# Entry writes behind the slot's last values, block 0's gather first, and products of zeros on TensorE in the loading phase and among the closing steps

## The chip, the cores and the metric

The kernel runs on one core of a Trainium2 chip, in one launch. The metric is the device time of an execution in microseconds; the median of three runs stands for a kernel. The engines are named as in the profile: PE (TensorE's products) and PEld (its weight loads), DVE (VectorE), ACT (ScalarE), POOL (GpSimd) and SP (SyncE, which here only starts transfers).

## The reference, cut to what matters

The input x is 128 sequences of 32 rows of 256 numbers; each sequence has a context of 257 rows. Six layers follow each other, each added to its input. LN is a layer norm without weights.

```python
x = x + cross_attention(LN(x), ctx)            # one head of 256, softmax, divided by sqrt(256)
x = x + causal_self_attention(LN(x))           # head of 128
x = x + ffn(LN(x))                             # 256 -> 1024 -> 256, quantised weights and activations, gelu
x = x + cross_attention_16_heads(LN(x), ctx)   # heads of 16
x = x + local_attention(LN(x))                 # each row sees two rows on either side
# mixture of experts on x_flat = LN(x), 4096 rows, 8 experts, 2 per row, capacity C = 1280
probs = softmax(x_flat @ router_w.T); top_v, top_i = top_k(probs, 2); top_v /= sum(top_v)
for k in range(2):
    pos = rank of the row among the rows that chose the same expert as k-th choice
    keep = pos < C
    y = gelu(x_row @ w1[e]) @ w2[e]
    out = out + y * (gate * keep)
x = x + out
```

All of it is in float32, apart from the quantised feed-forward layer, whose products run in bfloat16 on whole numbers.

## The kernel before

The 4096 rows are cut into 32 tiles of 128 rows (four sequences each). The kernel has two phases, each a block in which the five engines run programs of their own, tied by semaphores. Between the blocks stands a barrier that all engines pass together (L935).

**The tile phase** (`stack_phase`) is a software pipeline written out by hand. A loop over slots s = -6 ... 35 calls, on each engine, the steps of several tiles in a fixed order: `at(s + 3, c0_scores)` is the first cross-attention's scores of tile s + 3, `at(s, unit_values, 0)` the 16-head attention's values of tile s. That attention works in four units of one sequence each: scores (L1208), row maximum on DVE, exponential on ACT (L1390), transposes (L1216) and values (L1227). The values of a unit are 64 very short products of 128x32 weights with 16 columns, the densest stream of instructions that TensorE has. A unit's last key is not among its products: POOL multiplies it (`unit_last`, L1515) and selects each head's part (`unit_select`, L1520), and DVE adds both (`unit_own`, L808). Values 0 and 1 of a tile stand apart in the slot, values 2 and 3 directly behind each other.

**Routing** goes along in groups of four tiles. DVE works out, over four slots, for each row its two experts, its gates and its two places in a table in HBM. When a group's `place` is done, POOL writes the entries: one indirect DMA for each tile and choice, 128 entries of 8 bytes (`write_entry`, L1536). `tiles_scattered` says in which slot a tile's two writes come. The first five groups, tiles 0 to 19, are written in the tile phase, 40 writes in all; those of the last twelve tiles in the expert phase. In SP's slot 32, the wait for these 40 writes is followed by the load of the first table (`first_places`, L975), from which the first expert blocks take their rows.

**The loading phase** is the first 48 us or so. TensorE multiplies 20 products of zeros (L1024), waits for the first weights, folds Wq and Wk into one matrix (L1028, L1031) and then carries tile 0 through the first cross-attention (`c0_norm_T`, `c0_q`, `c0_scores`, ...), with further folds (`setup_folds`, L1044 and on) behind tile 0's output product. DVE scales and rounds the feed-forward weights in between (L1593, L1598). All the while the contexts of the first four tiles are loaded.

**The expert phase** (`expert_phase`) has 71 blocks of 128 rows, each with one expert: POOL gathers the rows (L2156), TensorE transposes them (`rows_T`, L2016), multiplies with w1 (`up`, L2038), ACT applies the gelu, TensorE multiplies with w2 (`down`, L2025), DVE scales with the gate, and POOL adds the result to the output (L2159). Its first steps are the *closing steps*: the last attention steps of tiles 28 to 31 are called here, woven into blocks 0 to 2. DVE begins with `s1_qT` of tile 30, for which TensorE's first step, `s1_v_scores`, waits; then it adds the last units of tile 31 (`unit_own`) and stages the row numbers of block 0 (`stage_from`, L1908). POOL first does a bias add and the router's inverse deviation and then gathers blocks 0 and 1. SP first starts the w1 weights of blocks 0 and 1 (1 MB each) and the last two experts' w2 (1 MB each).

```python
pe.wait_ge(zero_ok, 1)
for n in range(20):
    mm(ps[:, 6, 0:P], zero[:, 0:P], zero[:, 0:P], start=True, stop=True)
...
for t in tiles_scattered(s):          # POOL: scatter(s - 1, 0), then scatter(s - 1, 1),
    write_entry(t, k)                 # behind unit_select(s + 2, 1)
...
s1_v_scores(tiles - 2)                # TensorE, the first closing steps
unit_fold(tiles - 1, 2)
```

## Time and profile before

| | us |
|---|---|
| median of three runs | 1527.26 |
| lowest and highest | 1524.1, 1529.57 |
| the profiled execution, its own time | 1525.6 |
| its span, first to last instruction | 1523.8 |

| engine | busy us | share of the span | instructions |
|---|---|---|---|
| PE | 1415.4 | 93% | 19592 |
| PEld | 1207.9 | 79% | 19625 |
| DVE | 890.3 | 58% | 3143 |
| ACT | 837.6 | 55% | 2398 |
| POOL | 640.6 | 42% | 1195 |

The durations and times of day in this document are from the profiled execution; times of day count from its first instruction. The tile phase ends at about 961, the expert phase fills the rest. Two shares of the page mislead here. PE's 93% is an average over a phase that it fills and over stretches at half the clock, in which the same work counts double. And the chain that ended last, followed back from the end, names only the last write of the output and covers 0% of the span, so that what bounds must be read from busy times and waits. In the lines of the timeline the first number is the start, the second the length of a group of instructions, and in square brackets stands the idle time of the engine just before it with what ended it; "issue" means that no releaser is known.

### The profile page before, as it was taken

The numbers are of one execution on the slowest core, as the hardware profiler recorded it, in microseconds if no ns is written. First come the engines' busy times: TensorE is split into PE (matmuls) and PEld (weight loads), VectorE is DVE, ScalarE is ACT, GpSimd is POOL, SyncE is SP. The second block draws the span as 40 slices with busy tenths as digits, with TensorE's granted clock in tenths as the row PEclk, the third lists the DMA queues.
The fourth block names the chain that finished last, engine by engine and source line by source line (L and its number), as shares of the span: only waits on it lengthen the run. The fifth ranks groups of instructions, "written<-read, shape, count | busy, mean of one in ns | idle before, by whom it ended". The sixth has DMA issues, their size and how long they took to land. (4 is left out here: it accounts for less than half of the span.)

```text
span 1523.8 us, 51419 instructions
## 1 busy us (share of the span) xinstructions
PE 1415.4 (93%) x19592; PEld 1207.9 (79%) x19625; DVE 890.3 (58%) x3143; ACT 837.6 (55%) x2398; POOL 640.6 (42%) x1195
## 2 busy tenths in 40 slices
PE   6789999999999999999998988799899999999996
PEld 4467878777877777777777766699789999999996
DVE  4668889899988887887887786223211111111111
ACT  0488888888887887887887785322111111111110
POOL 1233444444444444444444343346633434443442
PEclk7999999999999999999999999799999999999999
DMA  9223434343333332332332222466556666666563
GB/s 338 113 68 101 119 98 119 96 123 100 104 105 100 103 96 89 102 107 89 96 99 75 68 86 106 174 172 175 147 171 177 187 187 173 177 186 187 173 176 75
DMA packets 91180, 199.47 MB, mean 131 GB/s; under 512 B 13568, under 2 KB 48128, under 8 KB 79840
## 3 DMA queue, kind: packets, MB, share of 16 engines
q1 hardware_dynamic: 72304, 174.68, 35.9%
q0 software_dynamic: 15680, 18.69, 7.0%
q10 hardware_dynamic: 2992, 3.28, 0.6%
q8 instruction: 140, 2.29, 0.6%
q14 instruction: 64, 0.52, 0.1%
HBM read 178.58 MB, written 18.29 MB: 129 GB/s over the span
## 5 line engine op out<-in xcount | busy, mean ns | idle before, releaser
L2111 ACT ACTIVATE heT<-ps 128x512 f32<-128x512 f32 x142 | 84.8, 597 | 428.3 <-PE ps L2038 401.5
L2038 PEld LDWEIGHTS ps<-xeT,w_block 128*128 128x128 f32 x2272 | 267.5, 193 | 13.5 <-issue 9.5
L2038 PE MATMUL ps<-xeT,w_block 128*128 128x128 f32 x2272 | 269.3, 277 | 9.4 <-DMA w_block<-in_m_w 8.8
L1390 ACT ACTIVATE x_prob<-ps,x_nmax 128x257 f32<-128x257 f32 x512 | 237.3, 473 | 44.9 <-DVE x_nmax L1741 39.8
L2025 PE MATMUL ps<-contexts,heT 128*128 x1136 | 257.0, 379 | 1.6 <-DVE ye L1921 1.6
L2025 PEld LDWEIGHTS ps<-contexts,heT 128*128 128x128 f32 x1136 | 210.3, 190 | 27.6 <-issue 2.0
L1741 DVE TENSOR_REDUCE x_nmax<-ps 128x2 f32<-128x514 f32 x256 | 168.9, 681 | 21.1 <-PE ps L1208 21.0
L1216 PE MATMUL ps<-constants,x_prob 128*128 128x128 f32 x1024 | 159.9, 291 | 12.0 <-ACT x_prob L1390 10.4
L1394 ACT ACTIVATE x_probT<-ps 128x512 f32<-128x512 f32 x256 | 147.2, 631 | 7.4 <-PE ps L1216 6.4
L1920 DVE COPY to_ix<-places 128x1 uint32 x71 | 10.9, 154 | 233.9 <-PE ps L2025 231.3
L1216 PEld LDWEIGHTS ps<-constants,x_prob 128*128 128x128 f32 x1024 | 121.5, 148 | 29.9 <-ACT x_prob L1390 26.2
L1227 PEld LDWEIGHTS ps<-contexts,x_probT 128*32 128x32 f32 x8192 | 97.3, 110 | 59.4 <-issue 36.4
L2153 POOL TENSOR_TENSOR rt_hold<-constants 128x1 f32<-128x1 f32 x145 | 34.8, 240 | 247.5 <-DVE ye L1921 120.3
L1227 PE MATMUL ps<-contexts,x_probT 128*32 128x16 f32 x8192 | 105.4, 185 | 29.0 <-issue 27.9
L2159 POOL DMA_INDIRECT out<-ye,to_ix x71 | 113.5, 1598 | 28.8 <-issue 24.0
L1390 ACT ACTIVATION_READ_ACCUMULATOR x_prob<-ps,x_nmax 128x1 f32 x512 | 103.2, 202 | 0.0
L1515 POOL TENSOR_TENSOR x_lastv<-contexts,x_prob 128x64 f32<-128x64 f32 x128 | 40.6, 317 | 135.9 <-ACT x_prob L1390 130.3
L1208 PE MATMUL ps<-contexts,query_blocks 32*64 32x257 f32 x2048 | 89.0, 403 | 5.4 <-ACT x_probT L1394 3.9
L1939 DVE COPY xeT<-ps 128x256 f32<-128x256 f32 x71 | 30.1, 424 | 97.0 <-PE ps L2016 97.0
L2156 POOL DMA_INDIRECT xe<-xnorm,from_ix x71 | 71.1, 1002 | 22.7 <-issue 20.2
L1520 POOL TENSOR_TENSOR x_select<-constants,x_rinv 128x8 f32<-128x8 f32 x128 | 27.4, 214 | 108.5 <-DVE x_rinv L1745 108.5
L1208 PEld LDWEIGHTS ps<-contexts,query_blocks 32*64 32x64 f32 x2048 | 30.2, 130 | 40.3 <-ACT x_probT L1394 23.5
(282 smaller groups left out, 2938.8 us busy)
## 6 DMA issues: line engine op xcount, KB each, us to landing
w_block<-in_m_w SPq DMA_DIRECT2D x71, 1024.0 KB
contexts<-in_cT SPq DMA_DIRECT2D x112, 257.0 KB, 3.0
contexts<-in_cn SPq DMA_DIRECT2D x112, 256.0 KB, 3.9
contexts<-in_m_w SPq DMA_DIRECT2D x8, 1024.0 KB, 6.9
contexts<-in_cT SPq DMA_DIRECT2D x4, 1028.0 KB, 11.7
xin<-in_x SPq DMA_DIRECT2D x32, 128.0 KB, 2.2
lastq<-in_lastq SPq DMA_DIRECT2D x32, 128.0 KB, 2.3
contexts<-in_cn SPq DMA_DIRECT2D x4, 1024.0 KB, 12.8
```

The costliest lines, as they stand in the source:

```text
L1208: i = mm(ps[h * HS:(h + 1) * HS, r, 0:KEYS], qblk[t % 2][r * GD:(r + 1) * GD, h, u, :, :].rearrange("p e q -> p (e q)"), cT[t % RING][r * ...
L1216: i = tr(ps[:, r, n * P:(n + 1) * P], p1[u % 2][:, r, n * P:(n + 1) * P], ident[:])
L1227: i = mm(b[rows_of, r * DH:(r + 1) * DH], p1T[u % 2][:, r, n, rows_of], cn[t % RING][:, u, n, lo:lo + DH], start=n == 0, stop=n == KT - 1)
L1390: A(p1[u % 2][:, r, :], ps[:, r, 0:KEYS], ACT.Exp, bias=nmax1[u % 2][:, r:r + 1], accum_out=rsum1[u % 2][:, r:r + 1]).then_inc(e1_ok.handl ...
L1394: A(p1T[u % 2][:, 2 * j:2 * j + 2].rearrange("p r k t -> p r (k t)"), ps[:, 2 * j:2 * j + 2, 0:KT * P], ACT.Copy).then_inc(t1_ok.handle, 1)
L1515: tt(lastv[u % 2][:].rearrange("p (r d) -> p r d", r=RG), lastk[t % RING][:, u, :].rearrange("p (r d) -> p r d", r=RG), p1[u % 2][:, :, KE ...
L1741: v_.tensor_reduce(nmax1[u % 2][:, 2 * j:2 * j + 2], ps[:, 2 * j:2 * j + 2, 0:KEYS], AX, ALU.max, negate=True).then_inc(m1_ok.handle, 1)
L2025: t = mm(ps[:, 3, 0:D], heT[b][:, k, :], w2[:, e, k, :], start=k == 0, stop=k == FK - 1)
L2038: t = mm(ps[:, half, at:at + P], w1[b][:, k, f * P:(f + 1) * P], xeT[b][:, k, :], start=k == 0, stop=k == H - 1)
L2111: A(heT[b][:, half * FK // 2:(half + 1) * FK // 2, :].rearrange("p k t -> p (k t)"), ps[:, half, :], ACT.Gelu).then_inc(heT_ok.handle, 1)
L2156: g.indirect_dma_start(xe[b][:], None, sources[round_of(u, n)], bass.IndirectOffsetOnAxis(ap=from_ix[b][:], axis=0)).then_inc(xe_in[b], 16)
L2159: g.indirect_dma_start(sums[round_of(u, n)], bass.IndirectOffsetOnAxis(ap=to_ix[b][:], axis=0), ye[b][:], None, compute_op=ALU.add).then_i ...
```

## The change

Entry writes: POOL's two calls of `scatter` become calls of `scatter_behind`, at two places of the slot: behind `unit_select(s + 1, 3)`, with a wait until TensorE has finished values 3 of that tile, and behind `unit_select(s + 2, 1)`, with a wait for values 0 of tile s + 2. Both writes of a tile come together. `tiles_scattered` gives the first place to all tiles but tile 17, in slots first + 7 to first + 10 of a group; the fifth group is written in three slots, so that its last tile (19) comes in slot 29 and not in 31.

Block 0: DVE stages its rows before it adds units 2 and 3 of tile 31, and POOL gathers it before the bias add and the inverse deviation.

Products of zeros: `keep_busy(n)` issues n products of 128x128 zeros with 256 columns of zeros. In the loading phase these are 10 instead of the 20 narrower ones, 13 behind the first folds, and 3, 1, 1, 1, 1, 1 ahead of tile 0's steps of the first cross-attention. Among the closing steps they are 8, 3, 2, 2, 2, 6 and 2, 25 in all.

```diff
@@ -633,11 +633,14 @@
             if s - (first + n + ROUTED_BEHIND) == turn:
                 return g
 
-    def tiles_scattered(s):
-
-        for first, n in GROUPS[:IN_FIRST]:
-            for i in range(n):
-                if s == first + n + ROUTED_BEHIND + 4 + i:
+    def tiles_scattered(s, early):
+
+        for g, (first, n) in enumerate(GROUPS[:IN_FIRST]):
+            places = [(i, False) for i in range(n)]
+            if g == IN_FIRST - 1:
+                places = [(0, False), (0, True)] + [(i, False) for i in range(1, n - 1)]
+            for i, (turn, first_unit) in enumerate(places):
+                if s == first + n + ROUTED_BEHIND + 4 + turn and early == first_unit:
                     yield first + i
 
     def bank(n):
@@ -1020,8 +1023,11 @@
             mm = nc.tensor.matmul
             tr = nc.tensor.transpose
             pe.wait_ge(zero_ok, 1)
-            for n in range(20):
-                mm(ps[:, 6, 0:P], zero[:, 0:P], zero[:, 0:P], start=True, stop=True)
+            def keep_busy(n):
+                for _ in range(n):
+                    mm(ps[:, 3, 0:D], zero[:, 0:P], zero[:], start=True, stop=True)
+
+            keep_busy(10)
             pe.wait_ge(fold_in, 48)
             for h in range(H):
                 for k in range(H):
@@ -1030,6 +1036,7 @@
                 for k in range(H):
                     t = mm(ps[:, 5, h:h + 1], setup_w["x0_Wk_T"][:, k, h * P:(h + 1) * P], cols["x0_bq"][:, k:k + 1], start=k == 0, stop=k == H - 1)
             t.then_inc(su_mm, 1)
+            keep_busy(13)
             pe.wait_ge(consts_loaded, 16)
             pe.wait_ge(su_first, FIRST)
 
@@ -1067,12 +1074,16 @@
                 i.then_inc(pe_s["cross0"].handle, 1)
 
             def c0_q(t):
+                if t == 0:
+                    keep_busy(3)
                 W(pe, act_s["cross0"], t, "normT")
                 for h in range(H):
                     i = product(bank(B["c0_q"])[:, h * P:(h + 1) * P], [(x0_A[:, k, h * P:(h + 1) * P], xnT["cross0"][:, k, :]) for k in range(H)])
                 i.then_inc(pe_s["cross0"].handle, 1)
 
             def c0_scores(t):
+                if t == 0:
+                    keep_busy(1)
 
                 m = t % RING
                 W(pe, act_s["cross0"], t, "q")
@@ -1087,6 +1098,8 @@
                     setup_scales()
 
             def c0_probs_T(t):
+                if t == 0:
+                    keep_busy(1)
                 W(pe, act_s["cross0"], t, "probs")
                 W_bank(pe, (t - 3, (o1_ok, 1)), (t - 1, (dve_s["self0"], "masked")))
                 for k in range(KT):
@@ -1094,6 +1107,8 @@
                 i.then_inc(pe_s["cross0"].handle, 1)
 
             def c0_values(t):
+                if t == 0:
+                    keep_busy(1)
 
                 W(pe, act_s["cross0"], t, "probsT")
                 for k in range(KT):
@@ -1102,12 +1117,16 @@
                 i.then_inc(pe_s["cross0"].handle, 1)
 
             def c0_att_T(t):
+                if t == 0:
+                    keep_busy(1)
                 W(pe, dve_s["cross0"], t, "att")
                 for h in range(H):
                     i = tr(bank(B["c0_att_T"])[:, h * P:(h + 1) * P], att[:, h * P:(h + 1) * P], ident[:])
                 i.then_inc(pe_s["cross0"].handle, 1)
 
             def c0_out(t):
+                if t == 0:
+                    keep_busy(1)
                 W(pe, act_s["cross0"], t, "attT")
                 product_in_halves(bank(B["c0_out"])[:, 0:D], [(attT["cross0"][:, k, :], full["x0_Wv"][:, k, :]) for k in range(H)]).then_inc(pe_s["cross0"].handle, 1)
                 if t == 0:
@@ -1535,10 +1554,12 @@
                     pool.wait_ge(waits_carried, g + 2)
                 nc.gpsimd.indirect_dma_start(table, bass.IndirectOffsetOnAxis(ap=place[:, t, k:k + 1], axis=0), entries[:, t, k, :], None).then_inc(table_in, 16)
 
-            def scatter(s, k):
-
-                for t in tiles_scattered(s):
-                    write_entry(t, k)
+            def scatter_behind(s, t_values, u_values):
+
+                for t in tiles_scattered(s, u_values == 0):
+                    W_if(pool, t_values, v1_ps, u_values + 1)
+                    for k in range(TOPK):
+                        write_entry(t, k)
 
             def slot(s):
                 at(s + 1, unit_select, 2)
@@ -1547,6 +1568,7 @@
                 at(s + 4, s0_rstd)
                 at(s + 4, s0_bias)
                 at(s + 1, unit_select, 3)
+                scatter_behind(s, s + 1, 3)
                 at(s + 2, unit_last, 0)
                 at(s + 2, q1_bias)
                 at(s, s1_bias)
@@ -1556,8 +1578,7 @@
                 at(s + 2, unit_last, 1)
                 at(s + 1, s1_rstd)
                 at(s + 2, unit_select, 1)
-                scatter(s - 1, 0)
-                scatter(s - 1, 1)
+                scatter_behind(s, s + 2, 0)
                 at(s + 3, q1_rstd)
                 at(s + 6, c0_rstd)
                 at(s + 4, ff_rstd)
@@ -1962,9 +1983,9 @@
                     dve.wait_ge(rt.tab_ok, 4)
 
             s1_qT(tiles - 2)
+            stage_from(0, 0)
             unit_own(tiles - 1, 2)
             unit_own(tiles - 1, 3)
-            stage_from(0, 0)
             stage_from(1, 1)
             unit_folded(tiles - 1, 2)
             s1_masked(tiles - 2)
@@ -2050,6 +2071,10 @@
             def expert(u, n=None):
                 return pe.value_load(tab_i[round_of(u, n)][0:1, bass.ds(u, 1)], min_val=0, max_val=EXP - 1)
 
+            def keep_busy(n):
+                for _ in range(n):
+                    mm(ps[:, 0, 0:D], zero[:, 0:P], zero[:], start=True, stop=True)
+
             def block_products(u, b, n=None):
 
                 up_part(u, b, 0, FK)
@@ -2064,14 +2089,21 @@
                 if is_at(u, 12):
                     table_rows_on_tensor(nc, pe, rt, const, 1, late_counts)
 
+            keep_busy(8)
             s1_v_scores(tiles - 2)
+            keep_busy(3)
             unit_fold(tiles - 1, 2)
+            keep_busy(2)
             unit_fold(tiles - 1, 3)
+            keep_busy(2)
             s1_probs_T(tiles - 2)
+            keep_busy(2)
             s1_values(tiles - 2)
             s1_out(tiles - 1)
+            keep_busy(6)
             rows_T(0, 0)
             ro_logits(tiles - 4)
+            keep_busy(2)
             up(0, 0, 2)
             s1_norm_T(tiles - 1)
             ro_norm_T(tiles - 3)
@@ -2194,9 +2226,9 @@
                 carrier()
                 add_rows(u, u % 2)
 
+            gather_block(0)
             s1_bias(tiles - 2)
             ro_rstd(tiles - 3)
-            gather_block(0)
             gather_block(1)
             s1_rstd(tiles - 1)
             s1_bias(tiles - 1)

```

Besides, `expert_phase` gets `zero` as an argument.

## Rows read from the trace of the kernel before

**Rows 1.** The page: granted TensorE clock in 40 slices, tenths of full speed.

```profile
PEclk7999999999999999999999999799999999999999
```

**Rows 2.** Windows of tile slots: length, busy per engine, clock, DMA share.

```profile
427.50:453.60 26.10, 25.73 (x508) 20.86 (x505) 24.06 (x85) 23.00 (x71) 11.43 (x27) 1.00 0.37 109
...
482.50:510.90 28.40, 26.45 (x501) 21.32 (x498) 23.91 (x86) 23.02 (x70) 13.45 (x29) 1.00 0.35 100
510.90:540.60 29.70, 27.86 (x506) 22.64 (x502) 24.18 (x87) 23.24 (x70) 13.28 (x29) 0.94 0.31 95
...
453.60:893.60 440.00, 409.28 (x7451) 333.20 (x7458) 362.06 (x1286) 347.11 (x1048) 198.94 (x419) 0.97 0.31 94
```

**Rows 3.** TensorE's waits, 140 to 960: total us, times, longest.

```profile
PE ps L1227 <- issue: 27.3, 55, 0.5
```

**Rows 4.** Timeline at 453: start, length, instruction, idle before.

```profile
453.87 1.18 POOL L1536 DMA_INDIRECT table<-rt_entries,rt_place  x1 [0.59 <-POOL rt_waiting L1534]
455.35 0.98 POOL L1536 DMA_INDIRECT table<-rt_entries,rt_place  x1 [0.30 <-issue]
...
453.55 0.54 PE L1227 MATMUL ps<-contexts,x_probT 128*32 128x16 f32 x39
454.40 0.28 PE L1227 MATMUL ps<-contexts,x_probT 128*32 128x16 f32 x5 [0.30 <-issue]
```

**Rows 5.** Timeline, weight loads just behind values 0, slot at 893.6.

```profile
896.35 0.14 PEld L1216 LDWEIGHTS ps<-constants,x_prob 128*128 128x128 f32 x1 [0.33 <-issue]
...
897.08 0.09 PEld L208 LDWEIGHTS ps<-constants,rt_tab 128*1 128x1 f32 x2 [0.39 <-issue]
```

**Rows 6.** Timeline at 415, the writes' new place: TensorE, POOL, DVE.

```profile
414.82 0.62 PE L1227 MATMUL ps<-contexts,x_probT 128*32 128x16 f32 x52
...
418.52 0.30 POOL L1515 TENSOR_TENSOR x_lastv<-contexts,x_prob 128x64 f32<-128x64 f32 x1 [4.01 <-ACT x_prob L1390]
...
423.55 0.20 POOL L1520 TENSOR_TENSOR x_select<-constants,x_rinv 128x8 f32<-128x8 f32 x1 [1.67 <-DVE x_rinv L1745]
...
420.78 0.69 DVE L1706 TENSOR_SCALAR ffn_hq<-ffn_hidden 128x1024 bf16<-128x1024 f32 x1
```

**Rows 7.** Timeline, last tile's values 2 and 3, last entry write.

```profile
955.62 0.65 PE L1227 MATMUL ps<-contexts,x_probT 128*32 128x16 f32 x41
...
960.48 0.85 PE L1227 MATMUL ps<-contexts,x_probT 128*32 128x16 f32 x67 [0.54 <-issue]
...
958.58 0.95 POOL L1536 DMA_INDIRECT table<-rt_entries,rt_place  x1 [0.30 <-issue]
```

**Rows 8.** Timeline, DVE's first step behind the barrier.

```profile
963.15 0.42 DVE L831 TENSOR_TENSOR self_qT<-ps,a_c 128x256 f32<-128x256 f32 x1 [6.91 <-PEq L935]
```

**Rows 9.** Timeline of the closing steps, TensorE.

```profile
963.63 2.07 PE L692 MATMUL ps<-w_a_Wv,self_normT 128*128 128x256 f32 x4 [2.29 <-DVE self_qT L831]
...
975.07 2.08 PE L2038 MATMUL ps<-xeT,w_block 128*128 128x128 f32 x8 [0.59 <-DVE xeT L1939]
...
978.45 1.06 PE L692 MATMUL ps<-self_normT,a_A 128*128 128x128 f32 x8
```

**Rows 10.** Windows of the loading phase, columns as in rows 2.

```profile
16.00:18.00 2.00, 0.00 (x0) 0.00 (x0) 1.02 (x4) 0.00 (x0) 1.46 (x3) 0.50 1.01 416
36.00:38.00 2.00, 2.00 (x15) 1.26 (x14) 2.00 (x2) 0.00 (x0) 2.00 (x3) 0.97 1.05 439
```

**Rows 11.** Timeline of the loading phase, TensorE and DVE.

```profile
9.05 1.99 PE L1028 MATMUL ps<-query_blocks 128*128 128x256 f32 x8 [1.19 <-DMA b_x_bq<-in_x_bq]
...
20.60 2.08 PE L692 MATMUL ps<-cross_normT,x_A 128*128 128x128 f32 x8 [1.82 <-ACT cross_normT L1310]
...
23.39 1.94 PE L1084 MATMUL ps<-contexts,cross_qT 128*32 128x257 f32 x16 [0.72 <-ACT cross_qT L1315]
...
28.12 1.28 DVE L1593 TENSOR_SCALAR x_probT<-x_probT,fw_inv 128x2048 f32<-128x2048 f32 x1
...
33.21 3.34 PE L1044 MATMUL ps<-x_outT,x_norm 128*128 128x256 f32 x8
```

More of the change, by code:

```diff
@@ L118, in build @@
             loop.close()
-            expert_phase(nc, closing, t_in, const, ps, xnorm, table, table_in, places, places_in, tab_i, rt, w2, w2_in, out, tiles, blocks, cap,
+            expert_phase(nc, closing, t_in, const, zero, ps, xnorm, table, table_in, places, places_in, tab_i, rt, w2, w2_in, out, tiles, blocks, cap,
                          sem, sig, sb_in(main))
@@ L1833, in stack_phase, with expert_phase @@
     return sync_steps, tensor_steps, scalar_steps, gpsimd_steps, vector_steps
-def expert_phase(nc, closing, t_in, const, ps, xnorm, table, table_in, places, places_in, tab_i, rt, w2, w2_in, out, tiles, blocks, cap, sem, sig, sb):
+def expert_phase(nc, closing, t_in, const, zero, ps, xnorm, table, table_in, places, places_in, tab_i, rt, w2, w2_in, out, tiles, blocks, cap, sem, sig, sb):
     ident = const["ident"]
```

## The prediction

> **What bounds the kernel now.** I read four views in this order: the page's clock line, the busy time cut at the tile slots, the waits of TensorE, and the timeline around what those waits name. The clock line shows two dips, in the first slice and in the 27th [rows 1]: the loading phase and the change from the tile phase to the expert phase. Between them and behind them TensorE is busy nearly all the time, so whatever lengthens its own work lengthens the kernel.
>
> A tile slot, from one tile's values of unit 0 to the next one's, lasts 26.10 us before the first entry write, with 25.73 us of TensorE work [rows 2]. The fifteen slots from 453.6 to 893.6 last 440.0 us, 48.5 us more than 15 × 26.10. Some last 28.40 us at full clock, others 29.70 us at a mean granted clock of 0.94 [rows 2]. The waits of TensorE name where this is lost: 27.3 us, in 55 pieces of at most 0.5 us, before products of the values (L1227) for "issue" [rows 3]. The timeline shows the cause. 39 of the 64 products of values 0 run at once, and as soon as POOL writes a tile's first entries the rest come in groups of about five with 0.3 to 0.5 us idle between them [rows 4]. So values 0 take some 3.2 us instead of 0.76, in all fifteen slots, each with one pair of writes. 2.4 us is the difference between 28.40 and 26.10 at full clock; the slots with a piece at 1.2 GHz lose 1.2 us more. Why POOL's write slows the issue of these short products no row tells. That the two belong together does not depend on it.
>
> The last tile shows it more strongly: 41 of 128 products run, the rest come only at 960.48, behind POOL's last writes, the final one at 958.58 [rows 7]. The barrier then lets DVE go only at 963.15, after 6.91 us idle [rows 8].
>
> **The change part by part.**
>
> *Entry writes.* The forty writes keep their count and length, 1.18 and 0.98 us [rows 4]. The first pair moves from beside tile 14's values 0 to behind tile 12's values 3, a slot and a half earlier (its places are ready a slot before that), and each pair gets a wait for the values just finished. Queued behind it on POOL are the last-key product of the next tile, the x1_bo and a1_bv bias adds, and the router's inverse deviation. For them DVE would wait. But POOL stands idle 4.01 us until 418.52 there, and the values end at 415.44 (414.82 + 0.62) [rows 6]. The pair needs 1.18 + 0.30 + 0.98 = 2.5 us [rows 4] and is done by about 418.2. If that cover is missing, POOL has 1.67 us of idle before its next selection [rows 6] before anything is late. I take nothing for it.
>
> What I remove is 48.5 us in the fifteen slots. About 2 us of it I leave standing, since the last three of them also hold the first block table's steps. What comes back is the effect of a write on other products. One pair of writes, the 17th, already falls just behind the values: the only traces are weight loads that come 0.33 and 0.39 us late [rows 5]. A full-width fp32 product there takes 133 ns per instruction (1.06 us for 8 [rows 9]), and five of the throttled ones take 0.28 us and then 0.48 idle, 150 ns each [rows 4], so long products hardly notice. Bounds: 0 and the whole 2.4 us per pair. I take 0.4, nearest to rows 5, and there are 17 such slots now (tiles 12 to 28): +6.8. **Sum −48.5 + 2 + 6.8 = −39.7 us.**
>
> *Last tiles.* Tile 19's entries are now written behind values 3 of tile 30, so nothing is written beside tile 31. Its values 0 lose their stall too, but ScalarE's exponentials bound that slot; I take −2 (bounds −3.5 and 0). Values 2 and 3 would end at 955.62 + 1.5 = 957.1, DVE's and POOL's last steps at about 956, and the barrier 0.3 us later: 957.4 instead of 963.1, **−5.7** (bounds −3 and −6). The read of the places leaves SP's last steps as well: its entries are there early.
>
> *Closing products of zeros.* Each is 128x256 in fp32; four such take 1.99 us at 2.4 GHz, 0.5 each [rows 11]. 8 + 3 + 2 + 2 + 2 + 6 + 2 = 25 of them are 12.5 us. In return the clock holds. Before it was 1.2 GHz from the barrier to about 978: the first value products 2.07 us, block 0's first products 2.08 for 8 where 1.06 is the price at 2.4 GHz [rows 9]. From 963.1 to the last tile's query product at 978.45 passed 15.3 us. TensorE's real work between these, at 2.4 GHz, I estimate at half of what stands there, 7.6 us. With 12.5 it makes 20.1 without a gap: **+4.8 us**, all passed on, because what follows is one chain through ScalarE. The first eight alone hold back value products that could have started 0.5 us behind the barrier. Bounds: 0, if the waits were long anyway, and +8.
>
> *Block 0's gather first.* DVE stages its rows behind one step instead of five, POOL gathers without the two steps before it, some 1.5 us earlier. But the zeros put TensorE at block 0's transpose 15.8 us behind the barrier, where the rows were there at 10 already (block 0's products began at 975.07 [rows 9]). Nothing, with bounds 0 and −1.
>
> *Loading.* Ten 256-column zeros replace twenty of 128; they end before the weights (9.05 [rows 11]). Thirteen more run from 11.8 to 18.3, and the first transpose needed 18.1: 0.3 late at most. In that gap TensorE stood idle and its clock fell: 0.50 from 16 on, until 36 to 38 [rows 10]. With the zeros I expect 2.4 GHz there. On the chain of tile 0 this saves 1.0 us in the query product (2.08 at 1.2 GHz [rows 11], 1.06 for the same form at 2.4 [rows 9]), 0.8 in the scores (1.94), 1.3 in the folds (3.34 for the form that took 1.99 at 9.05) and, by the same ratio, about 1.0 in the output product and 0.5 in two transposes [rows 11]: 4.6 us, less the 0.3. The values' saving of 0.9 is not in it, since DVE's scaling of the feed-forward weights (1.28 us, until 29.40) holds the step behind them [rows 11]. The single zeros between the steps fit into waits of 0.5 us and more. The rest of the chain to tile 0's first unit is latency and shifts with it. **−4.3 us** (bounds −5.5 and +3, if the clock falls anyway and the zeros are late).
>
> **Sum.** −39.7 − 2 − 5.7 + 4.8 − 4.3 = −46.9. The profiled execution took 1525.6 us (span 1523.8, 1.8 around it), so 1478.7; the median of the runs shown is 1.7 above it, which gives 1480.
>
> **A rule weighed.** DVE's long steps beside the new place are a reduction and, from 419.5 on, two steps on the hidden row; the writes should be done by 418.2. The Trainium skill, SBUF — State Buffer, "SBUF: two separate sides", says that a VectorE operation in a 2-port mode locks GpSimd out while it would write the descriptors of its own DMAs. By that rule a late pair of writes would be held until those steps end. No row here shows such a hold, the writes lasting 1.0 to 1.2 us everywhere.
>
> **Rivals.**
> - *The stall moves with the writes* (0.09): every pair costs its 2.4 us in the value and score products that now stand behind it, without the falls of the clock. For it: the products behind values 3 are dense too, with no idle time of TensorE to take the stall. Against: rows 5 and their length. 17 × 2.4 = 40.8 instead of 6.8 gives 1514.
> - *The closing runs at 1.2 GHz in spite of the zeros* (0.06): the work and the zeros take 40 us instead of 20. For it: TensorE's idle time at the barrier. Against: the dense work up to it. 1480 + 20 = 1500.
> - *POOL's writes run long* (0.03), held until the last of DVE's steps on the hidden row ends at 421.5 (420.78 + 0.69 [rows 6]): POOL is late by 3.3 us, 1.7 above its slack, × 17 = 29 us: 1509. Against: 1.3 us lie between the writes' end and these steps. This is where the Trainium skill's rule above would lead.
> - *Slower* (0.03): a pair stops the issue for its whole 3.2 us behind the values, so that nothing at all runs in the 3.2 us, and the clock falls (1.2 us) in each slot: 17 × 4.4 = 75 instead of 6.8, so 1548. It decides from 3.2 us per pair on, where 54 us of gain are used up.
> - *The change does little of what it says* (0.02): the writes still meet values, because the wait passes late and the next ones are near. About 1526.
>
> **How the numbers follow.** The forecast has 0.77. Its own range is 1468 to 1492: 0 to 0.8 us per pair (±7), loading (−1, +7), closing (±5), added as independent. 8 in 10 need a little of the first two rivals: 1466 to 1498. A measurement of this kernel tells 0.3%, 4.6 us, from no change. Faster by more: 0.77 + 0.09 + 0.06 + 0.03 = 0.95; within: 0.02; slower 0.03.
>
> **What would show it.** In the trace after: values 0 at 0.7 to 0.8 us throughout and no "issue" wait at L1227; slots 12 to 28 at 26.1 to 26.8 us and no clock below 2.4 GHz in them; POOL's writes ending before the next last-key product; a barrier within half a microsecond of TensorE's last value product; 2.4 GHz from 12 to 36 us and tile 0's first unit some 4 us earlier; 12.5 us of zeros in the closing and the last tile's query product about 20 us behind the barrier. It is wrong if slots 12 to 28 stay above 27.5 us, or if the closing's clock is 1.2 GHz.

## The result, and the profile after

On the chip of the first measurement the changed kernel takes **1468.26 us** (median of 4 runs, 1468.01 to 1472.68) where the kernel before takes 1527.93 (4 runs, 1524.1 to 1529.57): a ratio of 0.962, 95% interval 0.959 to 0.965. 1480 was forecast, with a range of 1466 to 1498. The profiled execution took 1468.07 us, its span is 1466.2.

That number holds for that chip. In three of the four later series, on four chips, the kernel *before* took 1474, 1478 and 1477 us. In one of these the whole change was run again, and it is worth 0.3% there (below). In the fourth series the kernel before took 1523. Whether the fourth is the chip of the first measurement isn't known. The two levels don't overlap: 61 runs lie between 1468.2 and 1482.4, and the fourth series' 11 between 1517.8 and 1531.8. This section compares the two traces of the first measurement.

Clock line of the page, after (answers to [rows 1]):

```profile
PEclk9999999999999999999999999999899999999999
```

Windows of the trace after, cut at the same events as the prediction's steps (start and end, length, busy us and instructions of PE, PEld, DVE, ACT, POOL, clock, DMA share, GB/s): start to values 0 of tile 0; slots 0 to 11; slots 12 to 28; slots 29 and 30; last tile to barrier; barrier to block 0's down products; the rest.

```profile
0.00:82.10 82.10, 64.10 (x466) 45.82 (x473) 47.90 (x129) 32.01 (x82) 18.17 (x41) 0.98 0.58 209
82.10:396.90 314.80, 307.06 (x5934) 248.16 (x5941) 279.41 (x945) 273.57 (x833) 133.91 (x307) 0.99 0.37 107
396.90:843.90 447.00, 438.27 (x8445) 355.50 (x8454) 409.35 (x1455) 390.03 (x1189) 227.00 (x477) 1.00 0.35 105
843.90:890.10 46.20, 38.92 (x855) 29.93 (x848) 35.08 (x127) 35.41 (x110) 21.45 (x45) 1.00 0.29 104
890.10:902.90 12.80, 10.29 (x313) 8.35 (x305) 5.01 (x19) 6.59 (x22) 0.97 (x4) 0.73 0.10 27
902.90:934.90 32.00, 29.53 (x187) 27.36 (x188) 9.89 (x42) 9.21 (x19) 9.11 (x18) 0.95 0.56 201
934.90:1466.20 531.30, 511.04 (x3496) 480.12 (x3494) 103.17 (x431) 88.49 (x145) 232.28 (x303) 0.99 0.60 169
```

The same stretches last 87.8, 313.6, 492.2, 50.4, 19.15, 29.15 and 531.5 us in the trace of before. The differences are −5.7, +1.2, **−45.2**, −4.2, −6.4, +2.9 and −0.2, which add up to −57.6, the difference of the spans. The third row is the change: 45 us less at a clock of 1.00, where it was 0.97 on the mean.

A slot in it, and TensorE's waits at the values from 140 to 960 us (answer to [rows 2, 3]):

```profile
475.80:502.00 26.20, 25.83 (x504) 20.88 (x501) 23.90 (x86) 22.94 (x70) 13.34 (x28) 1.00 0.37 108
```
```profile
PE ps L1246 <- issue: 2.3, 6, 0.6
```

27.3 us of issue waits in 55 pieces have become 2.3 in 6, and none of the six has a write beside it. The timeline shows a pair at its new place (answer to [rows 4, 6]): values 2 and 3 at 462.82, the writes behind them, and the probability transposes (L1235), which have a wait for ScalarE's exponentials there anyway:

```profile
462.82 0.97 PE L1246 MATMUL ps<-contexts,x_probT 128*32 128x16 f32 x88
...
464.10 1.05 POOL L1555 DMA_INDIRECT table<-rt_entries,rt_place  x1 [1.25 <-PE ps L1246]
...
465.45 0.96 POOL L1555 DMA_INDIRECT table<-rt_entries,rt_place  x1 [0.30 <-issue]
...
465.86 0.66 PE L1235 MATMUL ps<-constants,x_prob 128*128 128x128 f32 x4 [0.17 <-ACT x_prob L1409]
```

The end of the last tile and the closing steps (answers to [rows 7 to 9]; each product of zeros is two instructions in the trace, so x16 are eight of them):

```profile
901.21 1.32 PE L1246 MATMUL ps<-contexts,x_probT 128*32 128x16 f32 x128
902.87 3.69 PE L2076 MATMUL ps<-zero 128*128 128x256 f32 x16 [0.34 <-PEq L938]
906.40 1.03 PE L695 MATMUL ps<-w_a_Wv,self_normT 128*128 128x256 f32 x4
...
919.38 1.13 PE L695 MATMUL ps<-self_normT,a_A 128*128 128x128 f32 x8
...
927.07 0.70 PE L768 MATMUL ps<-self_val,self_probT 128*128 128x256 f32 x2 [1.75 <-ACT self_probT L882]
...
928.35 1.91 PE L2059 MATMUL ps<-xeT,w_block 128*128 128x128 f32 x8
```
```profile
902.87 0.42 DVE L834 TENSOR_TENSOR self_qT<-ps,a_c 128x256 f32<-128x256 f32 x1 [1.05 <-PEq L938]
```

Nothing interrupts the last 128 products of values, DVE waits 1.05 us at the barrier instead of 6.91, and a value product takes 1.03 us instead of 2.07. Behind 927 the clock falls once more: block 0's eight products take 1.91 us, after TensorE had idled 0.72 and 1.75 us.

The loading phase (answers to [rows 10, 11]), windows and TensorE's timeline:

```profile
16.00:18.00 2.00, 1.93 (x9) 1.35 (x8) 0.99 (x10) 0.00 (x0) 1.18 (x3) 1.00 1.00 409
```
```profile
12.07 5.86 PE L1028 MATMUL ps<-zero 128*128 128x256 f32 x26
...
20.81 1.16 PE L695 MATMUL ps<-cross_normT,x_A 128*128 128x128 f32 x8 [0.52 <-ACT cross_normT L1329]
...
22.69 1.07 PE L1095 MATMUL ps<-contexts,cross_qT 128*32 128x257 f32 x16 [0.28 <-ACT cross_qT L1334]
...
30.18 1.89 PE L1051 MATMUL ps<-x_outT,x_norm 128*128 128x256 f32 x8
```

### The profile page after: what moved, and what is told of

Read it like the earlier page. It is cut to its first block and busy times, and to the rows that moved or that the text cites. A ratio compares the mean times of both kernels' runs of the same rounds, so it can differ in the third digit from the quotient of the medians.

```text
span 1466.2 us, 51563 instructions
## 1 busy us (share of the span) xinstructions
PE 1399.2 (95%) x19664; PEld 1195.2 (82%) x19697; DVE 889.8 (61%) x3143; ACT 835.3 (57%) x2398; POOL 642.9 (44%) x1195
## 5 line engine op out<-in xcount | busy, mean ns | idle before, releaser
L1235 PE MATMUL ps<-constants,x_prob 128*128 128x128 f32 x1024 | 152.7, 282 | 12.2 <-ACT x_prob L1409 10.6
L2185 POOL TENSOR_TENSOR rt_hold<-constants 128x1 f32<-128x1 f32 x145 | 40.6, 280 | 255.8 <-DVE ye L1942 98.7
L1235 PEld LDWEIGHTS ps<-constants,x_prob 128*128 128x128 f32 x1024 | 114.7, 143 | 30.9 <-ACT x_prob L1409 23.6
L1246 PEld LDWEIGHTS ps<-contexts,x_probT 128*32 128x32 f32 x8192 | 90.6, 110 | 28.3 <-ACT ffn_hidden L1381 11.8
L1246 PE MATMUL ps<-contexts,x_probT 128*32 128x16 f32 x8192 | 93.7, 185 | 2.8 <-issue 2.3
```

The costliest lines, as they stand in the source:

```text
L1235: i = tr(ps[:, r, n * P:(n + 1) * P], p1[u % 2][:, r, n * P:(n + 1) * P], ident[:])
L1246: i = mm(b[rows_of, r * DH:(r + 1) * DH], p1T[u % 2][:, r, n, rows_of], cn[t % RING][:, u, n, lo:lo + DH], start=n == 0, stop=n == KT - 1)
L2185: g.tensor_tensor(hold[:], const["row"][:], const["row"][:], ALU.add).then_inc(carried, 1)
```

## The experiments

Twelve runs in four series, each series on a chip of its own; a ratio is to the kernel before on the same chip, with its 95% interval, and below 1 is faster. Series 1: `e1` to `e4`. Series 2: `e5` to `e7`. Series 3: `e8` to `e10`. Series 4: `e11` and `e12`. The expectations of the first two series were written when a before of 1527 was all that had been seen.

**e1, the moved entry writes alone.** The kernel before with these lines of the change and `tiles_scattered`, `scatter_behind` from it:

```diff
-                scatter(s - 1, 0)
-                scatter(s - 1, 1)
+                scatter_behind(s, s + 2, 0)
...
+                scatter_behind(s, s + 1, 3)
```

> The kernel before with the moved entry writes alone. Theory: the writes' stall of the values is nearly the whole gain, and the same stretches shorten as in the changed kernel: 45 us in slots 12 to 28, 4 in slots 29 and 30, 6 in the last tile and at the barrier, 55 to 56 us in all, so 1471 to 1473 us, values 0 at 0.76 us in every slot. Rival: the zeros in the loading phase and at the closing carry a large part (the clock is held by them), and the writes alone bring 40 us or less, 1487 or more.

Measured: 1468.44 us (before: 1474.04), ratio 0.9959 [0.9939, 0.9979]. The time lies 3 us below the forecast, but the forecast saving of 55 us is not there: the kernel before had no 50 us to give on this chip. That the time came out near is no sign for the theory's account of the saving.

**e2, the loading zeros alone.** `keep_busy(10)` for the twenty zeros, `keep_busy(13)` ahead of the wait for the constants, and the single ones in tile 0's steps.

> The kernel before with the products of zeros of the loading phase alone. Theory: tile 0's first values start 5.7 us earlier, at 82 instead of 88 us, and all of it stays: 1522. Rival: the gain of the loading is given back in the tile phase, since the additional instructions shift where TensorE's instruction blocks are loaded (the changed kernel lost 1.2 us between slots 0 and 12): 1524 or more.

Measured: 1474.65, ratio 1.0001 [0.9983, 1.0019]. Values 0 of tile 0 start at 81.2 (88.0 in the trace of before taken as `e9`). By slot 14 only 3.2 of these 6.8 us are left. Slot 0 is 1.6 us longer, but not by the zeros: it lasts 26.6 to 26.9 or 25.3 us in kernels with them and in kernels without them (26.65 in the first trace of before, 25.29 in `e9`). Six of the slots 7 to 13 are 0.1 to 0.8 us longer, with 1.1 to 1.7 us for values 1 in them and no write of entries near.

**e3, the closing zeros alone.** The seven `keep_busy` of the closing steps, nothing else.

> The kernel before with the products of zeros among the closing steps alone. Theory: they hold TensorE's clock at 2.4 GHz but cost more than they bring: the stretch from the barrier to block 0's w2 products grows from 29.1 to about 32 us, 3 us slower in all, 1531. Rival: behind the long idle time at the old barrier the clock does pay, and the kernel is 2 us or more faster, 1526 or less.

Measured: 1479.82, ratio **1.0045** [1.0029, 1.0062]: by themselves they cost 6.6 us by the ratio, 5.8 between the medians, about twice what was expected. The rival is refuted.

**e4, the change without them.**

> The changed kernel without the products of zeros among the closing steps. Theory: with the barrier early, TensorE comes to the closing steps a few us behind dense work, and without 10.8 us of zeros the steps from the barrier to block 0's w2 products take 29 us or less instead of 32: 3 to 5 us faster, 1463 to 1466. Rival: the clock falls to 1.2 GHz as in the kernel before and what the zeros cost they give back: 1468 to 1470.

Measured: 1470.77, ratio 0.9978 [0.9963, 0.9993]. Beside the 0.9967 of the whole change in series 3 that is no gain on the time. From the last values to block 0's down products 25.5 us pass in the trace, where the changed kernel took 32.3, but the slots before it lost some 5 us to irregular pauses at the values, one of 1.81 us among them (shown below), so the total doesn't tell what the zeros cost.

**e5, the change with the writes not waiting for values 3.**

```diff
-                    W_if(pool, t_values, v1_ps, u_values + 1)
```

> The changed kernel without the wait for the values in front of the entry writes; their places in POOL's order are the new ones. Theory: the order of POOL alone doesn't keep writes and values apart. POOL is through with the selection of unit 3 about 1.2 us before values 3 end, so the first write starts beside values 2 and 3, and their 128 short products stall as before: about 2.4 us in each of 17 slots, some 40 us slower than the changed kernel, 1508. Rival: the place does it, the wait costs or brings nothing: 1468.

Measured: 1471.26, ratio 0.9966 [0.9948, 0.9983]. Beside the 0.9967 of the whole change that is the same time, so here the rival was right. The trace shows why this costs nothing here. The pair starts inside values 2 and 3:

```profile
752.33 1.76 PE L1246 MATMUL ps<-contexts,x_probT 128*32 128x16 f32 x120
...
752.81 1.05 POOL L1555 DMA_INDIRECT table<-rt_entries,rt_place  x1 [0.17 <-issue]
```

The two take 0.96 and 1.07 us instead of 0.74 and 0.73 (1.76 for 120 of the 128), and the slot still lasts 26.15, because behind them TensorE waits for ScalarE: those waits are 7.7 us in all here and 10.6 in the changed kernel. So the place behind values 3 has slack.

**e6, e7, plain copies at the old place.** The changed kernel, which besides copies each tile's two 128x2 entries to a scratch tensor where the old writes stood, by POOL's queue (e6) or by SP's (e7):

```diff
+        for k in range(TOPK):
+            eng.dma_start(scratch[t, k], entries[:, t, k, :]).then_inc(scratch_in, 16)
```

> The changed kernel, and at the old place of each tile's entry writes POOL also copies the same 2 x 128 entries to another tensor by plain transfers, without indices. Theory: what stalls TensorE's short products is POOL's making of a transfer's descriptors, of whatever kind, so values 0 take 2 to 3 us again in 20 slots: 30 to 50 us slower, about 1508. Rival: only the indirect form with its 128 places does it, and plain copies cost under 5 us: 1468 to 1473.

> The changed kernel, and beside values 0 of the same tiles SP copies the same 2 x 128 entries to another tensor by plain transfers of its own queue. Theory: the small transfers themselves don't disturb TensorE, only their making by POOL does: values 0 stay at 0.76 us and the time at 1468 to 1471. Rival: 256 transfers of 8 bytes slow the values whoever starts them: values 0 over 2 us, 1490 or more.

Measured: e6 1504.37, ratio 1.0198 [1.0136, 1.026]; e7 1489.31, ratio 1.0067 [1.0039, 1.0095]. Both theories missed. Waits of TensorE from 140 to 900 us, first e6, then e7:

```profile
PE ps L1260 <- issue: 12.4, 9, 2.7
```
```profile
PE ps L1264 <- issue: 11.4, 9, 2.4
```

And in e6's timeline the copies of slot 15 and a pause behind them:

```profile
478.45 1.21 POOL L658 DMA_DIRECT2D scratch<-rt_entries  x2
...
484.92 0.72 PE L1260 MATMUL ps<-contexts,x_probT 128*32 128x16 f32 x60
488.13 0.29 PE L1260 MATMUL ps<-contexts,x_probT 128*32 128x16 f32 x4 [2.49 <-issue]
```

Values 0 right beside the copies are whole. But in five (e6) and six (e7) of the fifteen slots 14 to 28 TensorE stops once for 1.3 to 2.7 us, mostly in values 1. The stop begins 7.1 to 8.2 us behind the start of the copies. It does so whichever queue carries the copies, so POOL is not needed for a pause of this kind. The rest of e6's loss is its closing: 44.0 us from the last values to block 0's down products instead of some 32, with a wait of 10.7 us at the barrier. So e6 comes near the theory's 1508 by another cause. The wait is the experiment's own: POOL starts its last copies as late as 922.10 to 924.28, the edit lets it wait for all of them at the end, and it comes last to the barrier, at 935.7. These two kernels don't reproduce the stall of [rows 4], whose pauses are short, several, and inside the write.

What do such stops wait for? The packets of DMA queue q8, of the kind that the page calls "instruction", 16 KB each, give a lead. They come once in 6.6 us. e4 has a stop of the same kind without any copy or write beside it; its timeline, and then the whole DMA traffic from 860 to 864 us (GB/s in slices of 0.1 us):

```profile
863.63 0.30 PE L1246 MATMUL ps<-contexts,x_probT 128*32 128x16 f32 x11 [1.81 <-issue]
```
```profile
GB/s 0 0 0 0 0 0 0 0 0 0 164 0 0 0 0 0 0 0 0 0 0 0 0 0 0 0 0 0 0 0 0 0 0 0 0 0 0 0 0 0
q8 instruction: 1, 0.02, 1.8%
```

One packet starts at 861.07 and ends at 862.21, and 1.42 us later the products go on. The traces of all kernels but the first one of before show 77 "issue" pauses of TensorE above 0.15 us between 140 and 900 us. 76 of them end 1.26 to 1.60 us behind the end of such a packet, the long stops of e6 and e7 among them. So the irregular pauses fit a TensorE that has used up its instructions and waits for the next block of them. This is a match in time and not an experiment: no run moved the blocks alone. The stall of the first trace is something else: of the three or four pauses in each of its values 0 at most the first one follows a packet so closely, and no packet lies between the pauses.

**e8 and e9, both kernels again.** Unchanged copies, in one series on a third chip, the kernel before with a profile.

> The changed kernel itself, beside the kernel before on one chip. In the first two series the kernel before took 1474 and 1478 us where the prediction's pair of measurements had 1527. Theory A: what the old place of the entry writes costs depends on the chip (2.7 us a slot in the trace of before, 0.0 to 0.4 us in the trace of the closing-zeros kernel, which has them at the same place). Then, if this chip is like those, the ratio is 0.995 to 1.002 (1466 to 1478 us): the moved writes give 6, the loading zeros nothing to 6, the closing zeros cost up to 6. If this chip is like the first one, both numbers of the first measurement come back: before 1527, ratio 0.962. Theory B, the rival: the chip has no part in it, and the kernels with one edit each were spared the stall because their code lies differently. Then before must show 1527 here with the stall in its trace, or a ratio near 0.962, whatever the chip.

> The kernel before, for a trace of it on this chip. Theory A: with a time of 1474 to 1478 the first values of slots 14 to 28 last 0.76 to 1.2 us, not 3.0 to 3.5, no stretch of these slots is at half clock, and the slots are 26.1 to 26.6 us long as in the closing-zeros kernel, the clock staying at 1.0. Theory B: the values last 3.0 to 3.5 us and the time is 1527.

Measured: e8 1471.30 (1467.12 to 1476.68, 12 runs) beside a before of 1477.14 (17 runs), ratio **0.9967** [0.9949, 0.9986]; e9, one execution, 1472.94. So the small ratio is no matter of partial edits: it is the same pair of kernels on another chip. Windows of e9 (slots 14, 16, and 14 to 28), and its timeline at values 0 of slot 14:

```profile
452.70:479.40 26.70, 26.25 (x510) 21.51 (x507) 24.35 (x87) 23.14 (x70) 13.64 (x29) 1.00 0.36 106
505.60:531.80 26.20, 25.83 (x501) 20.89 (x498) 24.14 (x86) 22.92 (x70) 13.15 (x29) 1.00 0.36 108
452.70:847.30 394.60, 387.43 (x7451) 314.73 (x7458) 360.94 (x1286) 343.93 (x1048) 199.19 (x419) 1.00 0.34 105
```
```profile
452.72 1.20 PE L1227 MATMUL ps<-contexts,x_probT 128*32 128x16 f32 x64
...
453.04 1.18 POOL L1536 DMA_INDIRECT table<-rt_entries,rt_place  x1 [0.59 <-POOL rt_waiting L1534]
```

Beside [rows 2, 4] this is the finding of the study. The same instructions, the same write of 1.18 us, 0.32 us into the values in both; here the 64 products take 1.20 us, there 3.46. Fifteen slots take 394.6 us here and 440.0 there, and no slice of them is at a lower clock. The counts of TensorE's instructions in the two windows are equal (7451 products and 7458 weight loads in both).

What the moved writes still give on such a chip lies elsewhere than forecast. Slots 12 to 28 take 446.8 us in e9, 448.0 in e8 and 444.9 in e1. But from the last tile's values 0 to the barrier 17.3 us pass in e9 and 12.2 and 12.1 in e8 and e1: in e9 POOL's last four writes run until 906.9, the barrier opens at 910.5, and TensorE idles 6.22 us there, although its last 128 products take only 1.80:

```profile
902.99 1.80 PE L1227 MATMUL ps<-contexts,x_probT 128*32 128x16 f32 x128
911.01 2.07 PE L692 MATMUL ps<-w_a_Wv,self_normT 128*128 128x256 f32 x4 [6.22 <-DVE self_qT L831]
```

**e10, the second round's places loaded later.** e1, and:

```diff
-                if is_at(u, EARLY - 1):
+                if is_at(u, one[1]):
                     saved()
                     sp.wait_ge(table_in, TOPK * tiles * 16)
                     sp.dma_start(places[1][:], ...
```

> The kernel before with the moved entry writes and nothing else of the change, and with the second round's places loaded at block 30 and not at block 15. In the trace of after SP issues that load 17 us after the weights of block 15, because it waits for the last entries, and the weights of block 16 stand behind it: TensorE idles 8.5 us for them, at full clock before and at 1.2 GHz after. If that wait is all that is late there, this is 8 to 12 us faster than the kernel with the moved writes alone (1468.4 us beside a before of 1474.0), so 1457 to 1461 us or a ratio of 0.987 to 0.989. The rival: the products of block 15 and 16 wait next for something else (the late routing on VectorE, the gather), the gain is under 3 us and the ratio 0.994 to 0.997.

Measured: 1460.97, ratio 0.9893 [0.9868, 0.9919]. The wait in question, in the trace of e1 and then the same stretch in e10:

```profile
1045.30 5.21 PE L2043 MATMUL ps<-xeT,w_block 128*128 128x128 f32 x32 [8.69 <-DMA w_block<-in_m_w]
```
```profile
1041.29 3.62 PE L2030 MATMUL ps<-contexts,heT 128*128 x16
1044.74 3.73 PE L2043 MATMUL ps<-xeT,w_block 128*128 128x128 f32 x32
```

The idle 8.69 us and the slow products behind it (5.21 us for 3.73) are both gone. The three blocks around it take 21.7 us instead of 32.1, everything behind block 0's first down products takes 520.8 instead of 531.0, and the two ratios, each to before on its own chip, differ by 0.0066, 9.8 us. The wait was no limit of the transfer: SP stood at the places' load until the last entries were in, with the next block's weights behind it.

**e11, e12, the best versions.** e11 is e10 with block 0's rows staged and gathered first. e12 is the changed kernel without the closing zeros, with e10's edit; against e11 it adds only the loading zeros.

> The kernel before with the moved entry writes, the second round's places loaded at block 30, and block 0's rows staged and gathered first; no products of zeros. Against the same without the gather's move (ratio 0.9893 to before, 31.6 us from the last values to block 0's down products): theory, the gather is not what ends last, the ratio stays at 0.988 to 0.991. The rival: the kernel without closing zeros had 25.5 us there and the one with the writes alone 27.7, so the gather ends last and its move gives 2 us, ratio 0.986 to 0.988.

> The same with the zero products of the loading phase, and without those of the closing steps. In the kernels that have them the first values start 3 to 7 us earlier, but the slots behind lost 2 to 6 us of it again to longer products of values. Theory: they bring nothing, ratio within 0.002 of the kernel without them. The rival: what they gain at the start (5 us, 0.3%) stays, ratio 0.984 to 0.986. If the late load of places is worth the same 10 us in this code as in the other, it is 0.0066 below the 0.9978 of the kernel without closing zeros, so 0.991.

Measured beside a before of **1523.04** (11 runs): e11 1460.98, ratio 0.958 [0.9547, 0.9612]; e12 **1457.27** (1453.96 to 1458.32), ratio 0.9561 [0.953, 0.9591]. Here the kernel before is back at 1523, the writes at their new place cost nothing, and both versions come out as they would elsewhere. e11 has no product of zeros at all and is 62 us faster. Take off the 9.8 us of the late places, and 52 are left for the moved writes and the gather, where the prediction had 47 for them (−39.7 − 2 − 5.7). So the first measurement's gain needs no zeros. That it is again the stall which before has here is concluded from its time; there is no trace of it. Slots 14 to 28 of e11:

```profile
454.40:847.90 393.50, 387.26 (x7472) 313.02 (x7462) 360.67 (x1288) 343.57 (x1048) 199.70 (x420) 1.00 0.35 105
```

The gather's move shows no gain (1460.97 without it, on another chip, so their ratios can't be compared). Yet TensorE does wait for block 0's rows in both, 1.49 us in e10 and 3.60 in e11, although POOL starts the gather 1.2 us earlier behind the barrier in e11. What lengthens that wait isn't shown. The loading zeros give 3.7 us between the two medians, with ranges that overlap (e11 from 1455.65 to 1463.52), so part of their gain at the start may stay. The two profiled executions can't tell: they also differ by 5.7 us in the closing, for its clock. e12 is the fastest kernel seen: 11 us below the first measurement of the changed one, and 14 below that of series 3, each on another chip.

## Why the prediction was right, step by step

*What bounds the kernel before* was read rightly for the trace it was read from: the loss beside the entry writes was real there, and it went with the writes. It was not a property of the kernel alone. The prediction gave a 0.95 chance to a gain by a cause that three of the four later chips hardly show. There, the right numbers are a before of 1475 and a gain of 0.3 to 0.4%, near its bound for no change, and the term of −39.7 is about nothing. The forecast came true because its measurement ran where the trace had been taken. For a claim about the kernel that is luck.

*The sum.* −57.6 us between the spans, −46.9 forecast: the steps were right in kind and nearly all too cautious. 1468.26 lies at the edge of the forecast's own range of 1468 to 1492. That range isn't what its terms give: ±7, −1 to +7 and ±5, added as independent, make 1471 to 1491, and the measured time is below that. A small slip besides: 28.40 less 26.10 is 2.3 and not 2.4.

*Entry writes, −39.7 forecast, −45.2 measured* (slots 12 to 28). The size of one term failed, that of what a pair costs behind the values, and not the mechanism. 0.4 us were taken. Slot 15 lasts 26.20, 0.1 above a slot without any write, because the pause of the transposes behind values 3 takes the rest (e5). 17 × 0.3 are 5.1 of the 5.5 us. The wait for values 3, which the prediction weighed as a risk, costs nothing, and on the one chip where its absence was tried, its absence costs nothing either. Whether it matters on a chip with the stall wasn't tried. No hold of a write shows: they last 1.05 and 0.96 us, where before had 1.18 and 0.98. The hold that the prediction weighed isn't tested by this, since the pair ends at 466.41 and DVE's steps on the hidden row begin at 467.83. Two of the signs named came out a little worse than said: slots 26 and 27, which also hold the block table's steps, last 27.2 and 27.1 us, and seven groups of values in slots 14 to 27 take 0.1 to 0.7 us more than they should, by pauses without a write beside them.

*Slots 29 and 30, nothing forecast, −4.2.* The prediction read the pair behind values 0 of slot 29 as harmless to long products [rows 5]. In that trace it wasn't: eight probability and table transposes there take 0.95 and 0.86 us, in after 0.60 and 0.60, and from values 0 to values 1 of slot 29 pass 7.1 us where after has 6.0. Another 1.6 us go from values 2 and 3 to the end of the slot, at a mean clock of 0.87 where after has 1.00, and 1.5 in slot 30. Here too the loss belongs to the stalled trace: e9, with the pairs at the same places, takes 25.1 and 20.8 us for the two slots, after 25.3 and 20.9.

*Last tile, −7.7 forecast (−2 and −5.7), −6.4 measured.* DVE starts 0.34 us behind TensorE's last products, as predicted; the slot's clock was 0.73 in after, which ate the rest.

*Closing zeros, +4.8 forecast.* Barrier to the last tile's query product: 16.5 us, 1.2 more than in before, and 20.1 were predicted. A zero costs 0.45 us and not 0.5, which is 1.3 us of the 3.6; the rest is real work that was estimated too high. A further 1.7 us were lost behind it, where the clock fell after a wait. Against the true alternative the step is worse than against before: e4, without zeros but with the writes moved, has 11.1 us behind the barrier (908.01 to 919.14) where the changed kernel has 16.5, so they delay by 5.4 us. On time, e3 shows +5.8 to +6.6 us. What they were to bring, the clock, e4 has without them, but not every kernel has. From the barrier to block 0's down products the five kernels with moved writes and no closing zeros take 25.1 (e4), 26.5 (e1), 27.2 (e12), 31.3 (e10) and 32.9 us (e11), at mean clocks of 1.00, 0.94, 0.94, 0.78 and 0.79. The four with the zeros take 30.5 to 32.0 at 0.95 to 1.00. So the zeros do hold the clock, at the price of what its fall costs at worst. The closing of e4, that of e11 and a wait in e11:

```profile
908.00:933.10 25.10, 18.22 (x136) 16.68 (x137) 9.83 (x42) 9.15 (x18) 9.20 (x18) 1.00 0.71 257
907.70:940.60 32.90, 23.98 (x137) 22.40 (x137) 10.00 (x42) 9.29 (x19) 9.15 (x18) 0.79 0.55 196
```
```profile
917.63 0.69 PE L2021 MATMUL ps<-constants,xe 128*128 128x128 f32 x2 [3.60 <-DMA xe<-xnorm,from_ix]
```

The clock falls in e11 at this wait for block 0's rows. Nor was the stalled last tile the whole reason why it was low in before: e9, without the stall, idles at the barrier for 6.22 us and has a mean clock of 0.74 behind it, as before has.

*Loading, −4.3 forecast, −5.7 measured in the trace.* The clock is 1.00 from 16 to 18 us and the query product, the scores and the folds take 1.16, 1.07 and 1.89 us, as listed. On the time the step is worth nothing in e2 and 3.7 us in e12. What eats it is irregular: pauses of 0.2 to 0.8 us at values in slots 7 to 28, which the kernels without these zeros have hardly (e9: one wait of 0.4 us from 140 to 890; e11: none; e12: 2.5 us in 7). They are the pauses that end behind a 16 KB instruction packet. More instructions ahead shift where the blocks begin, and that may be why they come with the zeros; no run shows it.

*Gather first, 0 forecast.* Right for the changed kernel, where TensorE, busy with zeros, never waits for block 0's rows. Without the closing zeros it waits for them in every trace (1.05 us in e9 to 3.60 in e11), and what the move is worth there isn't shown.

**What stays open.** Why a POOL write stretches the same 64 products to 1.2 us on three chips and 3.5 on the first (and, by its time, on the fourth series' one) isn't settled. What feeds TensorE with instructions doesn't tell: no q8 packet runs between the pauses of values 0 at 453.55, the last one before it ended at 453.19, and the packets take as long as in e9 (a mean of 0.86 and 0.84 us over both instruction queues). No partial edit with the writes in their old place ran on a chip with the stall. It may be the chip, or something that is fixed for a whole series on it. The two levels never mixed within one series, of 11 to 25 runs.

## What to carry to other kernels

A stall that the profile calls "issue" beside a small transfer may belong to the chip as much as to the kernel: measure both kernels on a second and third chip before giving the ratio, and keep the edit if it costs nothing where the stall is absent, as here (0.3 to 0.4% on three chips, 4% on the first). Put small scattered writes behind short dense products, where TensorE has a wait for another engine anyway. And before feeding an engine zeros to hold its clock, measure what the idle time costs and look for what causes it: here the zeros cost as much as the fall of the clock at its worst. A load with a long wait in a shared queue, like the places' ahead of the weights, was worth more (9.8 us) than all the zeros.

## What the runs showed of the hardware that was not expected

- One program, two levels of time by chip: 1468 to 1482 us (61 runs, three chips) and 1518 to 1532 (15 runs, the first measurement and series 4).
- Small plain copies of 128 × 2 words can be followed by one stop of TensorE of 1.3 to 2.7 us some seven microseconds later, with POOL's queue and with SP's (11 of 30 slots).
- A product of 128x256 fp32 zeros takes 0.45 us in a row of thirteen (5.86 us) and 0.46 in a row of eight (3.69).
- Runs of 64 to 128 short products pause by 0.2 to 0.8 us, once by 1.8, without a write of entries beside them, and 76 of 77 such pauses and stops end 1.26 to 1.60 us behind the end of a 16 KB packet of the instruction queue q8.
